# Two cross-attention layers on one core: the exponential of row-tile run 1 is taken ahead of rounding the next x

## What is computed

```python
q = heads(x @ Wq)                       # 20 heads of 16
k, v = heads(ctx @ Wk), heads(ctx @ Wv)
p = softmax(q @ k.T / sqrt(16))
x = merge(p @ v) @ Wo + b + x
```

## Time and profile before

| | us |
|---|---|
| three runs: median (lowest, highest) | 944.73 (940.63, 945.84) |
| profiled execution, time | 941.04 |
| its span | 939.2 |
| TensorE matmuls busy | 903.8 |
| VectorE busy | 686.2 |
| ScalarE busy | 544.1 |
| GpSimd busy | 400.0 |

### The profile page before, as it was taken

One profiled execution on the slowest core, in us unless ns is written; L12 is line 12 of the kernel. 1 busy time (PEld: TensorE's weight loads), 2 busy tenths in 40 slices (PEclk: granted clock), 3 DMA queues, 4 the chain that ended last, 5 costly groups with the idle time before them and its releaser, 6 DMA issues.

```text
span 939.2 us, 28086 instructions
## 1 busy us (share of the span) xinstructions
PE 903.8 (96%) x11518; PEld 685.7 (73%) x11518; DVE 686.2 (73%) x1223; ACT 544.1 (58%) x547; POOL 400.0 (43%) x227
## 2 busy tenths in 40 slices
PE   8899999999999999998999999999999999999797
PEld 5777778777777877776677687777778777777564
DVE  4776786867678686686768778786787878677456
ACT  4456565656666565565466656566565656656452
POOL 3433354624435453365443456354344625422223
PEclk9999999999999999999999999999999999999999
DMA  6313434544453544544455444444544544444342
GB/s 212 89 34 93 132 99 113 142 127 132 104 142 90 160 133 120 139 117 121 122 145 140 106 108 128 132 131 123 132 107 110 132 128 133 113 116 98 94 107 84
DMA packets 80526, 112.41 MB, mean 120 GB/s; under 512 B 21200, under 2 KB 37878, under 8 KB 80400
## 3 DMA queue, kind: packets, MB, share of 16 engines
q1 hardware_dynamic: 80400, 110.61, 44.3%
HBM read 60.24 MB, written 22.24 MB: 88 GB/s over the span
## 4 chain that ended last, share of the span: by engine, by line
PE 49%; DMA 17%; SPq 15%; DVE 8%; issue 6%; ACT 3%; POOL 1%; DVEq 0%; ACTq 0%; POOLq 0%
PE pR L306 18%; PE pR L432 8%; PE pA L379 6%; SPq L1389 6%; PE pR L366 5%; DMA X<-y 5%; DMA X<-in_xT 4%; DMA y<-X 4%; PE pR L286 2%; SPq L1359 2%; SPq L1396 2%; DMA out<-X 2%; PE pR L256 2%; SPq L1423 2%; ACT P L742 2%
## 5 line engine op out<-in xcount | busy, mean ns | idle before, releaser
L742 ACT ACTIVATE P<-pA 77x2048 f32<-77x2048 f32 x160 | 300.3, 1877 | 166.8 <-PE pA L385 166.6
L993 DVE TENSOR_REDUCE Mx<-pR 128x4 f32<-128x308 f32 (+1 forms) x480 | 258.9, 575 | 32.7 <-PE pR L366 27.5
L1252 POOL TENSOR_TENSOR On<-On,OS 128x1024 f32<-128x1024 f32 (+1 forms) x58 | 105.7, 1844 | 276.7 <-DMA OS<-rd 276.6
L306 PE MATMUL pR<-OS,Wo 128*128 128x512 f32 x638 | 170.1, 406 | 4.1 <-DVE OS L1049 3.3
L306 PE MATMUL pR<-XS,Wq 128*128 128x512 f32 x638 | 168.5, 403 | 2.7 <-POOL Wq L1238 1.6
L432 PE MATMUL pR<-P,VA 77*17 77x256 f32 x2480 | 156.8, 383 | 2.2 <-DVE Mx L993 1.6
L366 PEld LDWEIGHTS pR<-KH,QH 32*128 32x128 f32 x1280 | 96.5, 183 | 78.2 <-issue 43.7
L366 PE MATMUL pR<-KH,QH 32*128 32x154 f32 x1280 | 132.0, 284 | 15.4 <-ACT P L742 7.4
L379 PE MATMUL pA<-QH,KH 32*77 32x256 f32 x1280 | 145.6, 292 | 0.1
L306 PEld LDWEIGHTS pR<-OS,Wo 128*128 128x128 f32 x638 | 114.7, 189 | 34.6 <-issue 4.8
L306 PEld LDWEIGHTS pR<-XS,Wq 128*128 128x128 f32 x638 | 116.3, 189 | 31.8 <-POOL Wq L1238 2.0
(11 more groups left out here) (154 smaller groups left out, 1215.2 us busy)
## 6 DMA issues: line engine op xcount, KB each, us to landing
On<-Oraw SPq DMA_DIRECT2D x248, 64.0 KB, 2.7
OS<-rd SPq DMA_DIRECT2D x58, 256.0 KB
C<-in_cT SPq DMA_DIRECT2D x16, 616.0 KB, 8.0
X<-in_xT SPq DMA_DIRECT2D x16, 512.0 KB
y<-X SPq DMA_DIRECT2D x16, 512.0 KB, 4.2
X<-y SPq DMA_DIRECT2D x16, 512.0 KB
out<-X SPq DMA_DIRECT2D x15, 512.0 KB, 4.2
X<-in_xT SPq DMA_DIRECT2D x16, 256.0 KB
```

The source lines that it names most:

```text
L306: f = pe.matmul(p[:, :], W[:, k, c0:c0 + 128], S[:, s, :], start=(i == 0), stop=(i == len(pairs) - 1))
L742: act.activation(P[0:L, i % PR, :, :], pA[0:L, :, :], ACT.Exp, scale=float(D) ** -0.5).then_inc(p_done, 1)
L993: dve.tensor_reduce(Mx[:, :, :].rearrange("p t (j i) -> p j t i", j=4)[:, j:j + banks, :, i:i + 2], pR[:, bank:bank + banks, 0:2 * LK].rea ...
L1252: pool.tensor_tensor(On[rows, blocks, :], On[rows, blocks, :], recips(u, part).bitcast(F32), ALU.mult).then_inc(o_mul, 1)
```

## The change

In the even units 2 to 28 of ScalarE's list, `S(u, 1)` is issued ahead of `split_x(u + 2)` where it was issued behind it. All other lists, buffers, semaphores and counts are the same.

```diff
                     elif u < NU - 2:
                         K(w, 1)
                         Q(u + 1, 1)
+                        S(u, 1)
                         split_x(u + 2)
-                        S(u, 1)
                         if u < NU - 4:
                             v_half_copy(w)
                         if u == NCH - 2:
```

## The result

The changed kernel took 954.63 us (median of four runs, 954.30 to 956.63), the kernel before 945.29 in the runs beside it; the ratio is 1.011, with an interval of 1.0074 to 1.0145. It is slower, by about 1.1%. The profiled executions lie 13.4 us apart: 954.42 against 941.04, spans 952.6 against 939.2.

What follows compares the result with a forecast made beforehand. TensorE's instruction list was taken to set the time. Ordinary units +7.5, unit 12's clock -1.5, unit 14 -0.7, unit 28 +3.1 and meetings +4.0 gave +12.4 us on 941.04, so 953.4 us, range 945 to 960.

Steps and rivals of the forecast that it cites:

- R: Reference moment in a unit: run 1 is done on TensorE and out(z, 0) starts.
- The place and size of the new wait: Even units, query product Q(u + 2, 2): TensorE waits 1.07 us for x's remainders, starting at R + 7.18 instead of R + 6.11.
- The twelve ordinary units: Units 2 to 12 and 16 to 26: new waits +12.8 us, less 5.3 of removed run 2 waits, net +7.5.
- unit 12's clock: Unit 12: the half-speed clock behind run 2's 1.69 us wait goes away, -1.5 us.
- The meetings of GpSimd and VectorE: GpSimd's L1252 pair blocks VectorE's L917 in two of units 10, 22 and 26, 2.0 us each: +4.0.
- Unit 28: No V(w, 2) here: query product 1.6 us later, plus 1.5 of clock loss behind one long wait, +3.1 together.
- the clock term: Unit 28: a wait of 2.5 us in one piece lowers TensorE's clock, +1.5 us.
- Unit 14: Query product also waits for new Wq's remainders, +0.7 us; its GpSimd and VectorE meeting nearly stops costing, -1.4; together -0.7.
- the removed waits are won: Even units: run 2's 7 waits for run 1's exponential, 7.4 us in all, go and count as gain.
- The rival of late x: Late landings of x hide most of the loss: old kernel 945 us, new 946 to 949, within 0.5%; chance 0.20.
- the clock falling at every new wait: Rival: each of twelve new 1.07 us waits is followed by 1.5 us of clock loss, 971 us; chance 0.08.

Runs made afterwards that it cites:

- the second profile: The changed kernel, nothing further altered, run and profiled again on another chip: 960.7 us, ratio 1.0191 to the kernel before.
- run 2: Not a follow-up: the part of a unit's TensorE list after out(z, 0) and V(w, 2), which in even units waited for run 1's exponential in the kernel before.
- run 1: Not a follow-up: the part of a unit's TensorE list ahead of out(z, 0), whose scores ScalarE's exponential takes; it is done at R.
- the covered kernel: The changed kernel with K(w, 2) ahead of Q(u + 2, 2), their banks exchanged and K's copies and sums ahead of Q's: 939.3 us, ratio 0.9967.
- one place later still: The changed kernel with split_x(u + 2) moved behind the copy of half of V in even units: 1002.4 us, ratio 1.064.
- the first swap: The changed kernel with K(w, 2) ahead of Q(u + 2, 2) in TensorE's even units, banks not exchanged: 949.8 us, ratio 1.0062.

## Why the prediction was right

It gave 953.4 us, in a range of 945 to 960, slower with 0.73; measured 954.63. It counted from the profiled execution of the old kernel, 941.04, to which it added 12.4; between the profiled executions the change is 13.4, between the medians 9.3. Point by point, with the two profiled executions set side by side at R and at the start of K(w, 2) in each even unit:

- **The place and size of the new wait.** Forecast: rounding at R + 1.82, remainders at R + 7.13, query product at R + 7.18 whatever x does. Measured R + 1.82, R + 7.09 and R + 7.15 in unit 8, and the last within 0.06 us in 12 of 14 units. The runs that cover or stretch this wait bear out that it, and the meetings that come with it, are the cause: 1.1 us of work put ahead of it, with banks and copies exchanged, turned 1.019 into 0.997 on the same chip (0.995 on a second), and 1.8 us more of it gave 1.064.
- **The twelve ordinary units.** Forecast +7.5 and -1.5 for unit 12's clock, 6.0 together. Measured +8.2. Behind a wait the five matmuls of the query product took 1.45 us instead of 1.30, which was not in the sum and is most of the difference; unit 6's late x adds 0.6. Unit 12 alone went by -2.0 (forecast 1.07 - 1.69 - 1.5 = -2.1), and its clock held:

```profile
389.00:393.00 4.00, 3.22 (x29) 2.44 (x29) 2.39 (x5) 1.33 (x3) 0.72 (x1) 1.00 0.46 156
```

- **The meetings of GpSimd and VectorE.** Forecast +4.0, two meetings at 2.0 each in units 10, 22 or 26. Four came, in units 12, 16, 20 and 22; the stretches behind them grew by 0.3, 2.2, 1.1 and 1.6, 5.3 us together. Unit 16, the largest: GpSimd began 0.35 us ahead of L917, held VectorE for 3.55, and TensorE waited 1.77.

```profile
513.60 3.72 POOL L1252 TENSOR_TENSOR On<-On,OS 128x1024 f32<-128x1024 f32 x2 [4.91 <-DMA OS<-rd]
513.95 3.55 DVE L917 SCALAR_TENSOR_TENSOR KL<-Kt,mask,KH 128x154 fp32r<-128x154 f32 x2
...
518.46 0.34 PE L366 MATMUL pR<-KH,QH 32*128 32x154 f32 x2 [1.77 <-DVE Mx L993]
```

  The mechanism was right. The sum came near by two errors against each other: too few meetings, and 2.0 each where these four cost 1.3 on average. (Three of the second profile cost about 3 us each, with their clock.) The list of units was mostly wrong, only 22 was on it. The working let GpSimd's pair start where it had stood in its unit; but in unit 16 it began at R + 14.25 before and at R + 12.00 after, so the DMA that it waits for landed 2.25 us earlier behind R, for a reason that was not traced. Which units meet differs between two profiles of the same program. One reading was wrong as well: the short instructions held in unit 14 were L907, with one tensor operand (Kt), and not "such" instructions as the sentence of the Trainium skill cited there speaks of. The case with two, L917, is shown first by the new profile: 2.80 to 3.55 us instead of 0.66.
- **Unit 28.** Forecast +3.1, of it 1.5 for the clock. Measured +1.6: the clock term did not come (1.00 in the stretch from 848 us). The wait was not in one piece: run 2 waited 1.08 for L1060 and the query product 1.25. This term failed.

```profile
844.91 0.34 PE L366 MATMUL pR<-KH,QH 32*128 32x154 f32 x2 [1.08 <-DVE X L1060]
...
848.90 1.43 PE L306 MATMUL pR<-XS,Wq 128*128 128x512 f32 x5 [1.25 <-POOL XS L1220]
```

```profile
848.00:852.00 4.00, 3.10 (x25) 2.44 (x29) 2.01 (x5) 1.23 (x3) 0.85 (x1) 1.00 0.38 122
```

- **Unit 14.** Forecast -0.7. Measured +1.1 up to K(w, 2), and -0.5 behind it, +0.5 in all: its meeting stayed (L907 was held 3.53 us), where the sum had it nearly gone.
- **The rest.** 8.2 + 5.3 + 1.6 + 0.5 is 15.6, and the profiled executions differ by 13.4. The other 2.2 are differences of -0.9 to +0.4 in stretches that the change does not touch, 0.9 of them behind unit 28. That the forecast came within 1.2 us of the median is partly luck: the meetings and the ordinary units were forecast 3.5 us too low and unit 14 1.2, unit 28 was 1.5 too high, 2.2 came off in stretches that nothing touches, and the old kernel's profiled execution lies 4.3 us below its median of 945.29.
- **Run 2's waits.** The step "the removed waits are won" hid something. In units 6, 10, 14 and 28 run 2 waited in the new profile too, for VectorE's L1060, 0.6 to 1.4 us. In units 6, 10 and 14 the reciprocal ahead of it waits for a late DMA, and with the reciprocal moved these waits went; unit 28's stayed, 0.94, so there the reciprocal is not the cause. It did not change the sum, since the query product waits until R + 7.15 anyway; in the covered kernel such waits take back 2.6 of 10 us.
- **The rival of late x** (within 0.5%) was wrong in these runs. So was the clock falling at every new wait: in ten units the query product had the whole wait of 1.04 us and run 2 none, and in each of them K(w, 2) started 1.25 to 1.3 us behind it, at full clock. The swing between two levels that the Trainium skill (TensorE: Matmul & The Clock Gate, A second HAM failure mode: psum-queue depth-cycling) reports for short, often repeated gaps, and that this rival cites, did not show here: with 13 waits of about 1 us the mean granted clock was 0.997. The falls behind waits of 2.7 us (one place later still) followed single longer waits and do not bear on it.

## What to carry to other kernels

Moving a step past another on one engine helps only one of the two chains that leave this engine. Before moving, write down for each chain when its last consumer gets there: here the exponential was needed at R + 3.2 and was late by 0.5 us on average, while x's remainders had 0.85 us to spare and lost 1.07. If the spare time is a little too short, look for work in the bound engine's list that doesn't need the result and can go ahead of it, and check which bank or buffer the moved work then holds longer: the first swap made some 10 us of waits that way, the second none. A shift of 1 us also changes which GpSimd and VectorE instructions meet.

## What was not expected of the hardware

- What a meeting holds VectorE for depends on whether the first of the two L917 slips through. In five meetings of the changed kernel's two profiles GpSimd's pair had begun 0.09 to 0.43 us ahead: the first L917 then took 2.1 to 2.5 us and the second 1.4, 3.44 to 3.77 together, each about as long as one operation of GpSimd's pair (2.4 and 1.34). In the other four L917 began 0.06 to 0.18 us ahead, or only 0.04 behind: the first L917 took its usual 0.37, the second 2.5, and both 2.80 to 2.83.
- The granted clock did not follow the length of a wait alone: 1.00 behind 1.04, behind unit 28's 1.08 + 1.25, behind 1.66 (second profile, unit 28) and 1.77 (first, unit 16), but 0.63 behind 1.93 and 0.57 behind 1.69 in the kernel before. With waits of 2.7 us it fell in most units but not in 2 and 6.
- The same program on another chip had a ratio of 1.019 instead of 1.011, outside the first interval. Five meetings instead of four, among them more long ones, go with it: the stretches behind the eight units that meet in either profile are longer by 8.5 us in sum, where the spans differ by 6.8. Why the DMAs landed so that more units met was not found.
